# Storing the output of an audio tower: indirect DMAs of GpSimd, one per tile, in place of SyncE's DMAs

## The reference

```python
h = tok(x)                              # interpolate, 255 windows of 64, |FFT|, soft minimum: (16, 255, 64)
h = h + attn0(layernorm(h))             # 8 heads, softmax(QK / sqrt(64)), output projection
h = h + ffn0(layernorm(h))              # 16 experts, top 2, relu, layernorm at the end
h = h + attn1(layernorm(h))             # 8 heads with a gated positional softmax
h = h + moe1(layernorm(h))              # y = tokens; for 8 experts: y += combine[e] * (gelu(tokens @ w1[e] + b1[e]) @ w2[e] + b2[e])
return h                                # out: (16, 255, 64) fp32
```

## Time and profile before

| | |
|---|---|
| median of three runs | 747.81 us (741.77, 747.81, 748.18) |
| span of the profiled execution | 745.7 us |
| TensorE busy | 652.7 us (88%), granted clock 0.948 of full |
| VectorE busy | 570.2 us (76%) |
| ScalarE busy | 502.8 us (67%) |
| GpSimd busy | 334.1 us (45%) |
| DMA | 24.37 MB, of which 1.31 MB written to HBM |

### The profile page before, as it was taken

One profiled execution on the slowest core, in us unless ns is written; L12 is line 12 of the kernel. 1 busy time (PEld: TensorE's weight loads), 2 busy tenths in 40 slices (PEclk: granted clock), 3 DMA queues, 4 the chain that ended last, 5 costly groups with the idle time before them and its releaser, 6 DMA issues.

```text
span 745.7 us, 16401 instructions
## 1 busy us (share of the span) xinstructions
PE 652.7 (88%) x4984; PEld 364.3 (49%) x4984; DVE 570.2 (76%) x1633; ACT 502.8 (67%) x1264; POOL 334.1 (45%) x417
## 2 busy tenths in 40 slices
PE   5528998999999988999999997699888988889896
PEld 5514654666666654323333324365555655565332
DVE  6676787777777774798999988669888888867653
ACT  3746877888888872576777767658777777744542
POOL 1006578788787875133333333725445644320000
PEclk9857999999999997999999999699999999987999
DMA  4030000000000001433333330000000000000001
GB/s 109 1 113 1 1 2 1 0 0 0 0 0 0 1 0 66 161 106 108 109 113 115 107 109 14 3 1 2 1 0 0 0 0 0 1 1 1 16 20 23
DMA packets 22038, 24.37 MB, mean 33 GB/s; under 512 B 12390, under 2 KB 12902, under 8 KB 21734
## 3 DMA queue, kind: packets, MB, share of 16 engines
q1 hardware_dynamic: 19751, 23.31, 10.3%
q10 hardware_dynamic: 2239, 0.49, 0.3%
HBM read 22.48 MB, written 1.31 MB: 32 GB/s over the span
## 4 chain that ended last, share of the span: by engine, by line
PE 59%; DVE 19%; issue 8%; ACT 4%; POOL 2%; DMA 1%; DVEq 0%; SPq 0%; ACTq 0%; POOLq 0%
PE ps L723 8%; PE ps L759 7%; PE ps L1551 5%; PE ps L641 4%; PE ps L1573 4%; PE ps L717 4%; DVE big L1091 4%; PE ps L652 3%; DVE big L2062 3%; DVE big L1132 2%; PE ps L1557 2%; PE ps L1802 2%; PE ps L709 2%; PE ps L1824 2%; PE ps L705 2%
## 5 line engine op out<-in xcount | busy, mean ns | idle before, releaser
L1338 POOL TENSOR_TENSOR big<-big 128x1024 f32<-128x1024 f32 x64 | 119.9, 1895 | 45.3 <-DVE big L1152 45.3
L939 ACT ACTIVATE big<-ps,big 128x255 f32<-128x255 f32 x256 | 117.3, 485 | 11.4 <-DVE big L1146 8.9
L901 ACT ACTIVATE big<-ps,b1s 128x512 f32<-128x512 f32 x128 | 80.3, 679 | 40.1 <-PE ps L641 38.9
L1146 DVE TENSOR_REDUCE big<-ps 128x4 f32<-128x1020 f32 x64 | 75.2, 1213 | 27.3 <-PE ps L717 27.3
L1920 ACT ACTIVATE big<-ps 128x1024 f32<-128x1024 f32 x64 | 65.9, 1030 | 32.9 <-PE ps L1563 30.5
L2062 DVE TENSOR_REDUCE big<-ps 128x4 f32<-128x1020 f32 x64 | 78.1, 1220 | 6.8 <-DVE res L2119 2.5
L723 PE MATMUL ps<-cst,big 128*128 128x128 f32 x512 | 77.5, 285 | 6.3 <-POOL big L1338 2.4
L1158 DVE COPY mid<-ps 128x512 f32<-128x512 f32 x96 | 63.5, 686 | 18.7 <-PE ps L723 15.4
L641 PE MATMUL ps<-big,wall 64*128 64x512 f32 x256 | 75.7, 656 | 0.7 <-ACT big L872 0.7
L723 PEld LDWEIGHTS ps<-cst,big 128*128 128x128 f32 x512 | 54.9, 141 | 40.8 <-issue 20.8
L652 PE MATMUL ps<-big,w2s 128*64 128x512 f32 x256 | 70.8, 632 | 1.2 <-ACT big L901 1.2
(11 more groups left out here) (274 smaller groups left out, 1342.2 us busy)
## 6 DMA issues: line engine op xcount, KB each, us to landing
mid<-spread_w SPq DMA_DIRECT2D x128, 128.0 KB, 2.8
mid<-in_split_sel SPq DMA_DIRECT2D x1, 1536.0 KB, 7.5
wall<-in_w SPq DMA_DIRECT2D x1, 1280.0 KB, 6.2
out_tokens<-res SPq DMA_DIRECT2D x16, 56.0 KB, 1.6
cst<-in_consts SPq DMA_DIRECT2D x1, 520.5 KB, 5.1
pexp<-in_w_raw SPq DMA_DIRECT2D x1, 512.0 KB, 6.2
w2s<-in_w SPq DMA_DIRECT2D x1, 512.0 KB, 3.4
mid<-in_taps ACTq DMA_DIRECT2D x1, 320.0 KB, 3.9
```

What stands on the lines that cost most here:

```text
L901: last = nc.scalar.activation(hid[e % 2][j], H1(e, j), ACT.Relu, bias=b1s[0][:, 2 * e + j:2 * e + j + 1])
L939: last = nc.scalar.activation(e_sb[r % 4][:, jj, tq, 0:NW], S[:, 2 * (r % 2) + jj, tq, 0:NW], ACT.Exp, scale=-1.0, bias=minus[r % 4][:, jj ...
L1146: nc.vector.tensor_reduce(minus[r % 4], S[:, 2 * a:2 * a + 2, :, 0:NW], AX.X, ALU.min).then_inc(s_mx, 1)
L1338: nc.gpsimd.tensor_tensor(e_sb[r % 4], e_sb[r % 4], bc(inverse[r % 4].unsqueeze(3), [P, 2, 2, 256]), ALU.mult).then_inc(s_A, 1)
```

## The change

GpSimd stores the output. `out` is seen as a list of 16 x 255 rows of 64 values. For tile t one indirect DMA writes each partition's row of `res[:, t]` to the row of `out` whose number stands in column t of `out_rows`, 128 rows for an even tile and 127 for an odd one. The numbers come with the constants as 32 more columns (partition p, tile t: p + 255 (t // 2) + 128 (t % 2)) and are turned into integers once, by a GpSimd copy after its last computing instruction. For each chunk GpSimd waits for `s_done` and issues four of these. SyncE only waits for all 32.

```diff
+        out_rows = sb("out_rows", [P, NT], U32)
...
+        o_rows = o_neg + 1
...
                 norm.root(pool, B - 2)
                 norm.root(pool, B - 1)
 
+                def store(t):
+                    n = P - t % 2
+                    place = bass.IndirectOffsetOnAxis(ap=out_rows[0:n, t:t + 1], axis=0)
+                    nc.gpsimd.indirect_dma_start(out.rearrange("b w d -> (b w) d"), place, res[0:n, t], None).then_inc(s_out, 16)
+
+                link_p(nc.gpsimd.tensor_copy(out_rows[:], cst[:, o_rows:o_rows + NT]))
+                for c in range(CH):
+                    pool.wait_ge(s_done, c + 1)
+                    for t in range(TC * c, TC * c + TC):
+                        store(t)
+
             @block.sync
             def _(sp):
-                def store(c):
-                    sp.wait_ge(s_done, c + 1)
-                    for tq in range(2):
-                        for first, n in ((0, 112), (112, 16 - tq)):
-                            src = res[first:first + n].rearrange("p (b t) d -> p b t d", t=2)
-                            sp.dma_start(out[bass.ds(2 * c, 2), P * tq + first:P * tq + first + n].rearrange("b w d -> w b d"),
-                                         src[:, bass.ds(2 * c, 2), tq]).then_inc(s_out, 16)
-
-                with sp.Fori(0, CH) as c:
-                    store(c)
-                sp.wait_ge(s_out, 16 * 4 * CH)
+                sp.wait_ge(s_out, 16 * NT)
...
+    rows = np.arange(P)[:, None] + (np.arange(NT) // 2 * NW + np.arange(NT) % 2 * P)[None, :]
+    return np.concatenate([a.reshape(P, -1).astype(f) for a in (ident, dft, iota, dist, sel1, neg, rows)], axis=1)
```

More of the change, by code:

```diff
@@ L2454, in constant_table @@
         neg[64 * j + ROWS:64 * j + ROWS + 2] = -1
-    return np.concatenate([a.reshape(P, -1).astype(f) for a in (ident, dft, iota, dist, sel1, neg)], axis=1)
+    rows = np.arange(P)[:, None] + (np.arange(NT) // 2 * NW + np.arange(NT) % 2 * P)[None, :]
+    return np.concatenate([a.reshape(P, -1).astype(f) for a in (ident, dft, iota, dist, sel1, neg, rows)], axis=1)
 def stack_table():
```

## The result

The changed kernel takes 773.73 us (median of five, 771.91 to 778.28), the kernel before 745.35 us in the same comparison: ratio 1.0396, 95% interval 1.0359 to 1.0434. It is slower by 28.4 us, and the forecast was +3.8. The experiments are compared with runs of the kernel before that were made together with them (medians of 745.4 to 746.1 us), and a time given without a ratio is of a single run.

The account below looks back on a forecast made before the run. TensorE was busy 88% of the span, but GpSimd idle during the stores and only a 3.3 us tail movable. Span 745.7 + 3.8 = 749.5, with 2.1 for the median 751.6 us; range for 8 in 10: 746 to 760.

Parts of the forecast that it names:

- Steps 1 to 3: Before the tail: load of 32 new columns 0 (0.16 us uncovered), GpSimd's integer conversion 0, stores moved from SyncE to GpSimd.
- Step 4: Tail after the last addition: eight GpSimd issues in a row from chunk 6 on, landing 747.7 against 743.9, +3.8 us.
- 1.02 us for 128x4 (line 465). I take that: In the tail: time taken for each indirect store's issue, 1.02 us, from another GpSimd instruction with little data.
- the bound of 1.89: Upper bound of the tail: 1.89 us per issue, backlog from chunk 5, landing at 756.3, +12.4 us.
- rival B: At the stores: odd tiles' 127 rows on one DMA engine, +2.0 to +7.4 us on top, 755.6 us; chance 18%.
- Step 5: Closing work after SyncE's wait stays as now: cost 0, bound another 1.8 us.
- Step 6: Packets of the stores: rows stay 256 bytes, 573 packets in the last stores' window stay about as many; cost 0.
- A: Store issues below 0.77 us leave no backlog from chunk 6; at 0.25 us -0.6 us, 747.2 in all; chance 12%.
- C: Store issues from 1.48 us on: last two chunks' backlog makes it over 1% slower; at 1.89 us 759.7 us; chance 17%.
- D: After chunk 0: GpSimd's stores stall VectorE, up to 2.9 us lost, 754.5 us with the forecast's tail; chance 4%.

## Why the prediction was wrong

**What bounds the kernel, and where the stores lie:** right. The change touched only the store; GpSimd was free; everything up to chunk 0's addition is the same work.

**Steps 1 to 3 (table, conversion, queues):** right. The load of constants has 536.5 KB and lands in 5.2 us instead of 5.1, the conversion takes 0.21 us at 683.9, and the first store comes 14 us later.

**Step 4 (the tail) failed.** The term that failed is "1.02 us for 128x4 (line 465). I take that", for all issues. For an even tile 0.98 us came close, by luck, since nothing ties line 465 to an indirect DMA. For an odd one it is 2.55 us, above even the bound of 1.89. The cost of an issue was bounded by the volume of other GpSimd instructions, and the row count of 127, which the prediction had seen, was priced as time of a DMA engine only (rival B), never as time of the program that writes the descriptors. That time goes by the rows of one share, 13.4 ns each. With it fell the path: the prediction let the backlog begin at chunk 6, and the stores have been late since chunk 2. The kernel with 128 rows shows that the rest of the picture held: backlog of eight issues, tail +5.5 us.

Three smaller terms were missing or mis-sized in the same step. The gap of 0.30 us between two issues, though the prediction had read a pitch of 0.58 at an issue of 0.33 in SyncE's rows. The landing: 3.6 us after the end of the last issue (127 rows) where 1.8 was taken; a store of 128 rows needs only 2.1 - 0.97 = 1.1 us. And the two gaps of 2.3 and 2.5 us. The bound from above, 1.89 us for every issue, is close to the true mean of 1.79, but it was put with a backlog of the last three chunks only. At 1.89 us four issues are 7.6 us against 6.45 a chunk, so by its own number the backlog begins with chunk 2, and the bound should have been 704.86 + 28 x 1.89 + 2.3 = 760.1, +16.2 and not +12.4. With 8.26 us a chunk the backlog grows over all that follow chunk 2: the tail is a sum over the stage, not over its end. The prediction's own method, with the pitch of 4.13 / 2 = 2.07 us from chunk 1 on (704.21 + 0.43 + 0.22), gives 704.86 + 28 x 2.07 + 1.8 = 764.6, +20.7 us; the long gaps (4.2) and the slower landing (1.8) make it +26.7. In the profile chunk 1's addition lies 39.7 us before the end of SyncE's wait in the kernel before and 67.3 in the changed one, +27.6; of the 0.9 us left, 0.6 is GpSimd's wait for chunk 2's addition.

**Step 5 (closing, cost 0)** came out for the changed kernel, 1.8 us in both, but by luck: GpSimd's drain at the end of the block wasn't thought of. It ends 1.9 to 4.9 us after GpSimd's last issue, and in the changed kernel the slow landing (774.6) just hides it (774.7). Where the landing is quick it shows: the closing stretch is 1.3 to 1.4 us longer with 128 rows and with GpSimd's plain DMAs, and 3.2 us longer with odd tiles in two parts.

**Step 6 (packets)** cost nothing that can be seen, but its reading was wrong: the stores were 19751 - 15167 = 4584 packets on SyncE's queue and are 2816 on GpSimd's.

**The rivals.** A (cheap issues) is wrong for indirect stores and right for plain ones, 0.55 us. B named the cause, 127 rows that can't be dealt out, and had the wrong place for it; its own effect is what SyncE's queue does with the same tiles, +3.0 us. C (dear issues) named the effect, "from 1.48 us per issue on", and gave 759.7; its argument against, that a store has only one index per row, was beside the point. D is shown, but at 0.97 us of the 2.9 it was priced at, and in a line just before those that were to show it: lines 2227 to 2237 (2225 to 2235 in the kernel before) take 2.15 us, as they did. The chance of 31% for slower by over 1% lay mostly on these two rivals, B and C, but no rival joined B's cause with C's effect, and so the range ended at 760.

## What to carry to other kernels

The issue time of an indirect DMA on GpSimd hangs on the divisors of its row count: here, for rows of 256 bytes, 0.85 us + 13.4 ns x (rows / largest divisor up to 16). So choose 128, 126, 120 or 112 rows. For 127 rows, a 128th that is dropped by a bounds check cost least of the indirect versions (ratio 1.0105 here); a second DMA for the rest cost more (1.0214). Price an issuing queue as throughput over the whole stage: if the issues of one step take longer than the step, the excess adds up over all of them and ends in the tail. And a plain pattern of addresses doesn't need a table: the same tiles by plain DMAs cost 0.55 us each at issue on GpSimd and 0.35 on SyncE.

## What I had not expected of the hardware

- 127 rows are dealt out in a plain DMA of GpSimd (0.55 us, 32 packets a tile) and not in an indirect one (2.55 us, 144 packets), and not in a plain one of SyncE (issue short, 18 GB/s).
- An indirect store of 127 rows has 7,620 bytes beyond its rows and semaphore writes, which is 4 bytes for each row on each of 15 engines.
- Where the sum of (rows of one share + 1) over the stores would pass a number between 980 and 1077, GpSimd pauses for 2.3 to 4.0 us before the issue.
- A VectorE instruction of 0.17 us took 1.10 us beside an issue of 2.56 us, and ended with it. Beside issues of 0.97 us the same line stayed at 0.17, and other VectorE instructions beside issues of 2.55 us were not stretched; which of them meet is open.
- GpSimd's drain at the end of a block ends 2.7 us after its last issue in three kernels (128 rows, and the two with plain DMAs of GpSimd), and between 1.9 and 4.9 us in the others.
